# Two stacked cross-attention layers on one core: last batch's layer 1 in two row halves, a small bias add on another engine, start rearranged, instruction orders replaced

## The reference

```
# layer 0 (softmax over the 512 query rows: axis=1)
q = x@Wq + bq;  k = ctx@Wk + bk;  v = ctx@Wv + bv
w = softmax(q @ k.T / 16, axis=1)
y = layernorm(w @ v + x) * gamma + beta
# layer 1 (softmax over the 1601 context rows)
Q = y@Wq1 + bq1;  K = ctx@Wk1 + bk1;  V = ctx@Wv1 + bv1
out = y + (softmax(Q @ K.T / 16) @ V) @ Wo + bo
```

## Time and profile before

| | |
|---|---|
| median of 3 runs | 480.08 us (479.08 to 480.79) |
| the profiled execution's own time | 478.87 us |
| its span, first to last instruction | 477.1 us |
| TensorE busy | 448.5 us (94%) |
| VectorE, ScalarE, GpSimd busy | 368.4, 385.3, 365.7 us |
| DMA | 17.29 MB, mean 36 GB/s |

### The profile page before, as it was taken

The page is one execution under the profiler, slowest core; times in us unless marked ns, Lnnn a source line. Parts: engine busy times, 40 slices in busy tenths (PEclk is TensorE's granted clock), DMA queues, the critical chain, the costliest instruction groups (busy, mean ns, idle before and its releaser), DMA issues.

```text
span 477.1 us, 7874 instructions
## 1 busy us (share of the span) xinstructions
PE 448.5 (94%) x2406; PEld 372.1 (78%) x2406; DVE 368.4 (77%) x892; ACT 385.3 (81%) x797; POOL 365.7 (77%) x322
## 2 busy tenths in 40 slices
PE   8798999999999999999999999999999998698786
PEld 8586667888878878888888878888888887585674
DVE  2689987788886988678886988678977986577844
ACT  3699799997999779997899879997899779952552
POOL 1567799978999689967998689967999589943400
PEclk9999999999999999999999999999999999999989
DMA  8400200021000210020100210011000010001001
GB/s 240 141 20 27 69 2 23 23 69 45 23 23 0 70 45 23 23 70 22 47 22 1 70 47 22 23 49 44 22 1 1 2 45 1 0 1 45 2 0 44
DMA packets 23896, 17.29 MB, mean 36 GB/s; under 512 B 1055, under 2 KB 23854, under 8 KB 23854
## 3 DMA queue, kind: packets, MB, share of 16 engines
q1 hardware_dynamic: 23850, 16.79, 11.5%
q10 hardware_dynamic: 4, 0.00, 0.0%
HBM read 12.59 MB, written 4.19 MB: 35 GB/s over the span
## 4 chain that ended last, share of the span: by engine, by line
PE 68%; DVE 13%; ACT 6%; POOL 6%; issue 6%; DVEq 0%; POOLq 0%; ACTq 0%
PE ps_s L773 10%; PE ps_s L627 9%; PE ps_s L629 8%; PE ps_s L628 8%; PE ps_l L627 7%; PE ps_l L629 6%; PE ps_l L628 6%; DVE max L1185 4%; ACT p L993 3%; PE ps_s L789 3%; POOL wsum L1299 2%; POOL p_lo L1306 2%; PE ps_l L660 1%; PE ps_s L741 1%; PE ps_l L824 1%
## 5 line engine op out<-in xcount | busy, mean ns | idle before, releaser
L1299 POOL TENSOR_TENSOR wsum<-wsum,p 128x512 f32<-128x512 f32 (+1 forms) x88 | 116.1, 1319 | 14.7 <-ACT p L956 14.4
L1306 POOL TENSOR_TENSOR p_lo<-p,p_hi 128x512 fp32r<-128x512 f32 (+1 forms) x91 | 117.4, 1294 | 4.2 <-ACT p_hi L964 4.2
L1118 DVE TENSOR_TENSOR p1T_lo<-ps_s,p1T_hi 128x512 fp32r<-128x512 f32 (+1 forms) x104 | 69.3, 685 | 25.0 <-ACT p1T_hi L1001 24.7
L950 ACT ACTIVATE p<-s_sb,min 128x512 f32<-128x512 f32 (+1 forms) x104 | 75.4, 726 | 13.6 <-issue 5.8
L1097 DVE CUSTOM_DVE_ANT_0 s_sb<-ps_l,cb 128x512 f32<-128x512 f32 (+1 forms) x104 | 70.4, 683 | 14.6 <-PE ps_l L629 9.8
L956 ACT ACTIVATE p<-p,r 128x512 f32<-128x512 f32 (+1 forms) x104 | 75.0, 724 | 4.2 <-DVE r L1104 3.7
L1001 ACT CAST p1T_hi<-ps_s 128x512 fp32r<-128x512 f32 (+1 forms) x104 | 58.2, 584 | 17.1 <-PE ps_s L773 14.4
L1185 DVE TENSOR_REDUCE max<-ps_s 128x1 f32<-128x804 f32 x60 | 58.4, 988 | 11.1 <-PE ps_s L629 10.0
L993 ACT ACTIVATE p<-ps_s,bias 128x1206 f32<-128x1206 f32 (+1 forms) x60 | 55.4, 926 | 11.9 <-DVE bias L1196 11.6
L773 PE MATMUL ps_s<-ident,p 128*128 128x128 f32 (+1 forms) x416 | 58.6, 277 | 5.7 <-ACT p L993 5.7
L964 ACT CAST p_hi<-p 128x512 fp32r<-128x512 f32 (+1 forms) x104 | 63.0, 621 | 0.5
(11 more groups left out here) (165 smaller groups left out, 1055.0 us busy)
## 6 DMA issues: line engine op xcount, KB each, us to landing
ctx_sb<-in_ctx_dram SPq DMA_DIRECT2D x24, 256.0 KB, 2.8
x_sb<-in_x_dram SPq DMA_DIRECT2D x8, 512.0 KB, 3.4
out_dram<-y_res SPq DMA_DIRECT2D x16, 256.0 KB, 2.2
p<-in_L_xattn_Wq_dram SPq DMA_DIRECT2D x2, 256.0 KB, 3.4
ctx_sb<-in_ctx_dram SPq DMA_DIRECT2D x8, 32.5 KB
p<-in_L_xattn_Wk_dram SPq DMA_DIRECT2D x2, 128.0 KB, 3.8
p<-in_L_xattn_Wv_dram SPq DMA_DIRECT2D x2, 128.0 KB, 4.1
p<-in_L_xattn_Wo_dram SPq DMA_DIRECT2D x1, 256.0 KB, 4.5
```

Source lines behind the costliest of these rows:

```text
L950: nc.scalar.activation(p0[0:m, ring0(i), :], s0_sb[0:m, (a + i) % 2, :], ACT.Exp, bias=min0[0:m, i:i + 1], scale=-1.0, accum_out=sum0[0:m, ...
L1118: nc.vector.tensor_tensor(p1T_lo[0:m, i % RING, :], ps_turn[i % 3][0:m, :], p1T_hi[0:m, i % RING, :].bitcast(F32), ALU.subtract).then_inc( ...
L1299: nc.gpsimd.tensor_tensor(total, total, p0[0:m, ring0(i), :], ALU.add).then_inc(wsum_done, 1)
L1306: nc.gpsimd.tensor_tensor(p0_lo[0:m, h, :], p0[0:m, ring0(i), :], p0_hi[0:m, h, :].bitcast(F32), ALU.subtract).then_inc(p0_lo_done, 1)
```

## The change

1. **Batch 7, layer 1, in two halves of the query rows.** After `exp1` of t = 0 and 1, `turn_p1_half`, `p1_turned_half`, `p1_low_half` and `weigh1_half` work on 256 of the 512 rows: 26 half tiles in place of 13 tiles. The rings for the split parts hold 8 half tiles. The sums of the halves have banks of their own (`ps_acc1h`), `weighed1_half` copies each, and `project_out` of batch 7 writes to banks of `ps_l0`. The three transpose banks are in `ps_s1`, so the scores of t = 0, 2 and 3 now all use `ps_l0` and only t = 1 uses `ps_s1`: t = 2 waits for `exp1` of t = 0, t = 3 for `exp1` of t = 2.
2. **Row bias of layer 1.** The second step of `bias_row1` (L1174, DVE) becomes `row_bias1`, an activation with a bias operand on ACT. All eight batches.
3. **The start.** The load of `wk0` is issued by ACT in front of its two small loads, with a semaphore of its own; the second and third group of `keep_warm` go; `turn_ctx(0, 0)` and `ctx_high(0, 0)` come ahead of the two small products; the first `weigh_u0` moves from POOL to DVE (`weigh_u0_first`), and `ctxT_low(0, 0)` comes behind it.
4. **All order tables are replaced.** Same steps, other order within a few places of the old one, in all three parts.

```diff
-WARM = (10, 2, 4)
+WARM = 10
-            return (ps_l0 if b == B - 1 and t % 2 else ps_s1)[:].rearrange("p (k m) -> p k m", m=BANK)
+            return (ps_l0 if b == B - 1 and t != 1 else ps_s1)[:].rearrange("p (k m) -> p k m", m=BANK)
+        HALF = T // 2
+        ps_acc1h = [s1_bank(3), ps_l0[:, 0:BANK]]
+            return ps_l0[:, (1 + h) * BANK:(2 + h) * BANK] if b == LAST else ps_out[h]
 # SP
-                sp.dma_start(wk_sb[0], wk0).then_inc(w_loaded[0], 16)
 # TensorE
-                before = t - 2 if b == B - 1 else t - 1
+                before = (None, None, 0, 2)[t] if b == LAST else t - 1 if t else None
+            def turn_p1_half(b, j):
+                h, i = j // MT, j % MT
+                if i == 0:
+                    pe.wait_ge(exp1_done, 2 * TB * b + 4 * (h + 1))
+                if j >= 3:
+                    pe.wait_ge(p1T_lo_done, MT * b + j - 2)
+                for k in range(2):
+                    mm = nc.tensor.transpose(ps_turn[j % 3][0:m, k * P:(k + 1) * P], p1[:, 2 * h + k, i * P:i * P + m], ident[:])
+            def weigh1_half(b, j):
+                pe.wait_ge(p1T_lo_done, MT * b + j + 1)
+                split3(ps_acc1h[h][:, 0:HALF], ctx_hi[b % 2][0:m, i, :], ctx_lo[b % 2][0:m, i, :], half_part(p1T_hi, m, j),
+                       half_part(p1T_lo, m, j), start=(i == 0), stop=(i == MT - 1)).then_inc(pv1_ps, 1)
             def project_out(b, h):
-                if h == 0:
+                if b == LAST:
+                    pe.wait_ge(at1_done, b + 1 + h)
+                    pe.wait_ge(exp1_done, 2 * TB * (b + 1))
+                elif h == 0:
                     pe.wait_ge(at1_done, b + 1)
 # TensorE, pre0
-                pe.wait_ge(w_loaded[0], 16 * 2)
+                pe.wait_ge(w_loaded[0], 16)
                 turn_wq(0, s1_bank(0))
+                pe.wait_ge(wk0_loaded, 16)
-                keep_warm(WARM[1])
+                turn_ctx(0, 0)        # now ahead of the two small products
-                turn_ctx(0, 0)
-                keep_warm(WARM[2])
 # ScalarE
+            def row_bias1(b, _):
+                act.wait_ge(c1_part_done, b + 1)
+                nc.scalar.activation(c1[:], c1_part[:], ACT.Identity, bias=c1_const[:, 0:1], scale=1.0).then_inc(c1_done, 1)
+            def p1_turned_half(b, j):
+                nc.scalar.copy(half_part(p1T_hi, m, j), ps_turn[j % 3][0:m, 0:HALF]).then_inc(p1T_hi_done, 1)
+            def weighed1_half(b, h):
+                act.wait_ge(pv1_ps, MT * (b + 1 + h))
+                nc.scalar.copy(at1[:, h * HALF:(h + 1) * HALF], ps_acc1h[h][:, 0:HALF]).then_inc(at1_done, 1)
+                act.dma_start(wk_sb[0], wk0).then_inc(wk0_loaded, 16)
 # VectorE
+            def weigh_u0_first(a, _):
+                dve.wait_ge(u0_done, 1)
+                nc.vector.tensor_tensor(xr[:], x_sb[0][:], u0_row[:].unsqueeze(1).broadcast_to([P, TB, E]), ALU.mult
+                                        ).then_inc(xu0_done, 1)
             def bias_row1(b, _):
                 dve.wait_ge(u1_part_done, b + 1)
                 nc.vector.tensor_reduce(c1_part[:], xr[:], AX_X, ALU.add).then_inc(c1_part_done, 1)
-                dve.wait_ge(c1_part_done, b + 1)
-                nc.vector.tensor_scalar(c1[:], c1_part[:], c1_const[:, 0:1], None, ALU.add).then_inc(c1_done, 1)
+            def p1_low_half(b, j):
+                nc.vector.tensor_tensor(half_part(p1T_lo, m, j), ps_turn[j % 3][0:m, 0:HALF],
+                                        half_part(p1T_hi, m, j).bitcast(F32), ALU.subtract).then_inc(p1T_lo_done, 1)
```

More of the change, by code:

```diff
@@ L276 @@
-    ("p0_low", 1, 11), ("p0_low", 1, 12), ("sum_weights", 2, 1), ("p0_low", 2, 0), ("ctx_low", 2, 0),
-    ("rsqrt_var", 1, 0), ("sum_weights", 2, 2), ("p0_low", 2, 1), ("rsqrt_var", 1, 1),
+    ("weigh_u0", 1, 0), ("ctx_low", 0, 0), ("ctx_low", 0, 1), ("sum_weights", 0, 1), ("sum_weights", 0, 2),
+    ("sum_weights", 0, 3), ("sum_weights", 0, 4), ("sum_weights", 0, 5), ("sum_weights", 0, 6), ("ctx_low", 0, 2),
+    ("sum_weights", 0, 7), ("sum_weights", 0, 8), ("sum_weights", 0, 9), ("sum_weights", 0, 10),
@@ L295 @@
[L295 to L299 removed]
[3 rows of a table removed]
+    ("rsqrt_var", 5, 0), ("p0_low", 6, 1), ("sum_weights", 6, 2), ("rsqrt_var", 5, 1), ("p0_low", 6, 2),
@@ L485, in xattn_kernel @@
         cols_loaded = [sem(f"cols_loaded{n}") for n in range(2)]
-        wv_loaded = sem("wv_loaded")
+        wk0_loaded, wv_loaded = sem("wk0_loaded"), sem("wv_loaded")
         rows_loaded = sem("rows_loaded")
@@ L756, in scores1 @@
                     pe.wait_ge(qw1_lo_done, b + 1)
-                before = t - 2 if b == B - 1 else t - 1
-                if before >= 0 and k in (0, len(chunks) - 1):
+                before = (None, None, 0, 2)[t] if b == LAST else t - 1 if t else None
+                if before is not None and k in (0, len(chunks) - 1):
                     pe.wait_ge(exp1_done, 2 * (TB * b + before) + (1 if k == 0 else 2))
@@ L788, in project_out @@
                     t = slice((2 * h + k) * P, (2 * h + k + 1) * P)
-                    mm = nc.tensor.matmul(ps_out[h][:, k * E:(k + 1) * E], at1[:, t], w2_sb[:], start=True, stop=True)
+                    mm = nc.tensor.matmul(out_bank(b, h)[:, k * E:(k + 1) * E], at1[:, t], w2_sb[:], start=True, stop=True)
                 mm.then_inc(out_ps, 1)
@@ L898, in pre0 @@
                 mm.then_inc(small_ps, 1)
-                turn_ctx(0, 0)
-                keep_warm(WARM[2])
             steps = {f.__name__: f for f in (
                 turn_x, project_q0, project_bias0, turn_ctx, scores0, weigh0, sum_rows0, predict, turn_y, project_q1, scores1,
-                turn_p1, weigh1, project_out, turn_w1, make_w1)}
+                turn_p1, weigh1, turn_p1_half, weigh1_half, project_out, turn_w1, make_w1)}
             pre0()
@@ L1273, in _ @@
             steps = {f.__name__: f for f in (
-                ctxT_low, xT_low, at0_low, bias_x0, q0_low, sum_z0, max0, recip0, residual0, moments0, normalised, bias_row1,
-                q1_low, rowmax1, bias1_of, recip1, p0_low_first, p1_low, finish, prepare_w1)}
+                ctxT_low, xT_low, at0_low, bias_x0, q0_low, weigh_u0_first, sum_z0, max0, recip0, residual0, moments0, normalised, bias_row1,
+                q1_low, rowmax1, bias1_of, recip1, p0_low_first, p1_low, p1_low_half, finish, prepare_w1)}
             pre0()
```

83 lines of the change are left out of this document (48 added, 35 removed), and 459 rows, old and new, of tables (GPSIMD_HEAD, GPSIMD_STEADY, GPSIMD_TAIL, SCALAR_HEAD).

## The result

| | before | after |
|---|---|---|
| median | 479.72 us (479.08 to 480.79, 4 runs) | 466.83 us (466.04 to 467.44, 4 runs) |
| ratio, 95% interval | | 0.9725 [0.9712, 0.9739] |
| the profiled execution, its span | 478.87, 477.1 | 466.4, 464.6 |

A forecast was written before the change was run, and what follows sets the result against it. The middle was taken as bound by PE's matmuls, with time to win at the ends. Tail 2.9, start 1.2, row bias 1.3 and tables 0.8 sum to 6.2 us: 480.08 to 473.9 us, 8-in-10 range 470.3 to 477.5.

The forecast's parts named there:

- those 3.6 us: Middle, 100 to 390 us: PE's idle time out of 290 us, the most a faster small step elsewhere could win.
- Tables: 0.8 taken: New order tables: 0.8 us won, mostly between 16 and 100 us; ends 9.4 won and a similar loss.
- Rival D: Order tables win half of the 9.4 us idle, 3.9 more than taken: 470.0 us; chance 0.12.
- Row bias: 1.3 taken: Small sum moved to ScalarE: counts only once, in layer 1 of batch 6, 1.3 us; ends 0 and 2.5.
- The term for batch 6: Layer 1 of batch 6, where PE waits for the exponentials: the small sum on ScalarE wins 1.3 us there.
- Tail: 2.9 taken: Last batch's layer 1 in halves: last weighing 2.5 us earlier, some 0.4 at the end; range 1.0 to 4.6.
- The lower bound: Tail: only 1.0 us won if matmuls pay at each change and the copies' queue costs another microsecond.
- Start: 1.2 taken: First batch: `project_bias0` at 14.7 in place of 15.87, 1.2 us won; ends 0 and 1.6.
- the rule that the throttled clock is the default state: Start without warm-ups: if the clock fell as in the tail, the sum would be 1.5 less, 4.7 us.
- A: GpSimd's steady order makes the second `rsqrt_var` 1.3 us late, layer norm sets the pace: 9.1 lost, 483.0 us; chance 0.07.
- B: Middle bound by matmuls, so gains of start and batch 6 are given back: 477.2 us; chance 0.14.
- C: PE waits for copies or the clock falls, so the tail brings 1.2, not 2.9: 475.6 us; chance 0.14.

The follow-up runs named there:

- a1: The kernel before with only the small sum (second step of layer 1's row bias) on ScalarE: 477.55 us, ratio 0.9954.
- m1: The kernel before with `ctxT_low` of the next batch moved ahead of `bias1_of` of t = 3 in VectorE's steady order: 482.74 us, ratio 1.0062.
- a4: The kernel before with only the new order tables of all four engines: 475.95 us, ratio 0.9927.
- m2: The kernel before with `q1_low` moved ahead of `bias_row1` in VectorE's steady order: 487.62 us, ratio 1.0150.
- t1: The kernel before with the new GpSimd tables alone, other engines' lists old: 507.96 us, ratio 1.0573.
- t2: The kernel after with GpSimd's old order, the first `weigh_u0` left with VectorE: 494.95 us, ratio 1.0312 to before.
- b4: The kernel after with the old order tables, only the new steps put in: 471.56 us, ratio 0.9827 to before.
- m4: The kernel before with the small sum on ScalarE and `ctxT_low` ahead of `bias1_of` of t = 3 in VectorE's steady order: 480.20 us, ratio 1.0012.
- s1: The kernel after with the second and third groups of warm-ups (12 passes) put back: 468.38 us, ratio 0.9765 to before.
- r1: The kernel before with `sum_weights` (c, 2) moved between the two `rsqrt_var` in GpSimd's steady order: 479.82 us, ratio 0.9999.
- a2: The kernel before with only the last batch's layer 1 in halves, its banks and tail order: 475.61 us, ratio 0.9922.
- b1: The kernel after with the second step of layer 1's row bias back on VectorE: 469.44 us, ratio 0.9792 to before.

## Why the prediction was too small

**Which step failed.** The one in the first part: "nothing in the change removes a matmul there; a faster small step on another engine can win at most those 3.6 us", and from it, in the part on the row bias, "In the middle the saving is off PE's path and counts nothing by itself". I read 99% busy as "bound by matmuls" and did not look at which waits made up the 1%. They were the same three in the steady batches, and one of them, 0.24 to 0.28 for `q1_low`, stood right behind the c step that the change takes from VectorE. a1 won 0.5 us a steady batch by that edit alone, about twice the listed wait. The middle's idle time fell from 3.6 to 1.2 us, where I had written that it would stay within 1.5 of 3.6. The 3.6 as a bound came out nearly right: of the 4.7 won, about 1 is the seven matmuls that moved on. But it is no safe bound, since the ends of matmuls are modelled and idle time is the least that PE waited: in m1 the same 289 matmuls show 53.76 us busy, in a4 52.95.

**Tables: 0.8 taken, 3.5 won alone, 4.9 lost when taken out.** I said that the trace has no row for it. It had the waits of 0.35 for `ctxT_low` and 0.24 to 0.28 for `q1_low`, four times each, 2.5 us. Rival D (half of the 9.4 us idle, 4.7) was near the case that came, and I gave it 0.12. But m1, m2, t1 and t2 show why no local reading of the tables could give a sign: one exchange costs 3 to 7 us, and GpSimd's list out of step with the others costs 28 us, whichever of the two sets is the others'.

**Row bias: 1.3 taken, 2.2 and 3.2 measured.** The term for batch 6, 1.3, was near: 1.0 in b4 and m4. What was missing is the steady batches, 0.5 us each with the old tables, which I had put at nothing. The cost on ScalarE, 0.3 us, was right: 0.285. The Trainium skill, "ScalarE: Activation LUTs", rules for kernel authors, gives additions to VectorE; the measurement decides against it for this size: 285 ns on ScalarE, a median of 1.17 us on VectorE beside GpSimd's work. The Trainium skill, "Perfetto Trace Analysis", Optimizing Scalar/DVE Operations, allows moving work to ScalarE if VectorE is saturated. VectorE was busy 77%, and the move won all the same, because of one place in its list.

**Tail: 2.9 taken, 3.5 in the trace, 3.7 and 3.8 by the ratios; the mechanism was right.** From the end of the exponentials of t = 1 (440.11) to the copy behind the last weighing (459.34) it took 19.2 us against 19.3 forecast. Two misses cancel in it. The gaps are 1.5 against my 2.2 (0.41, 0.85, 0.22; the third group of scores needs none), and the half tiles took 15.4 against my 14.8 if the scores of t = 3 took their 2.3: 0.59 each, not 0.57. The lower bound had named this with 0.02 us a change of kind, for which no row stood. The end behind the weighing gave 0.95 against 0.4 (6.21 to 5.26 us up to the end of the span), and that is where the 0.6 comes from: the eight matmuls of the two products ran as one train of 1.89 us that began 0.2 ahead of the copy, where I had counted 1.14 twice. The granted clock is 1.00 from 424.8 us on, and no wait of PE there after 440 us is above 0.85.

**Start: 1.2 taken, 1.5 to 1.8.** The single terms held: the product 1.22 on VectorE (1.25), `ctxT_low` 0.68 (0.7), both chains equal. `project_bias0` began at 13.84 against 14.7; over the six profiles with this start it is 13.69 to 14.84, so that after's is early is partly luck. The granted clock stayed at 1.00 without the warm-ups, and s1, which has them, is slower: the rule that the throttled clock is the default state (the Trainium skill, "TensorE: Matmul & The Clock Gate", Part 1), which I weighed against this edit, took nothing here.

**Last batch but one: 1.3 taken, 0.8, with seven matmuls more.** Idle time fell from 4.98 to 3.19, as forecast (to 4 or less). With the fifth batch, from which the seven came, it is 2.65: 1.45 with the small sum alone (b4 without the tables), 2.05 with the tables alone (a4).

**The rivals.** A did not come: PE shows no wait for xhat in after, and by r1 the second `rsqrt_var` is no later than it was. B (only the end counts) and C (the half tiles disappoint) are refuted by a4 and a2. The range ended at 470.3 because D was priced alone, without what the small sum won in the middle. No term stood for the second low stretch of the clock, which batch 6 of before has in part of its executions (last section); it is a likely source of the 1.2 us between the median and the profiled execution that the sum carried along unexplained.

**What stays open.** Which exchange in the new tables removes the wait for `ctxT_low`: the single exchange that stands in the new list did not by itself. The new list of one engine alone was tried only for GpSimd. How far the small sum and the tables help each other in the first batches rests on two profiles and on ratios whose intervals overlap. The profiled execution of b1 took 472.1 us, 2.7 above its median; behind the wait of 1.14 us it has a stretch at the low clock.

## What to carry to other kernels

A stretch that is 99% busy is not closed: list its waits and look for those that come back in every iteration, and whether the change touches the instruction ahead of the one they wait for; the step behind a wait of 0.25 us was worth 0.5 here, times the iterations. In a schedule written out over four engines, don't price one move by the wait it removes: ask what the engine would do in the hole (m2: it stood still for 1.56 us) and who is next behind (m1). Judge such tables as a whole, and measure a small step on another engine with the order it will have, since its gain can lie in the same wait as theirs, or in waits that only both remove.
